# A drain instruction raises TensorE's three increments in a counting sort that four engines share

## The reference, cut to what matters

```python
edge_mats = (bond_features @ W_bond + b_bond).reshape(-1, d, d)
h = atom_features
for _ in range(STEPS):                      # 4
    msg = jnp.einsum('eij,ej->ei', edge_mats, h[nbr])
    agg = jax.ops.segment_sum(msg, dst, num_segments=n_atoms)
    h = _gru_cell(agg, h, W_ih, W_hh, b_ih, b_hh)
...
deg = jax.ops.segment_sum(jnp.ones_like(edge_weight), col, num_segments=num_nodes)
norm = deg_inv_sqrt[row] * edge_weight * deg_inv_sqrt[col]
out = jax.ops.segment_sum(x[row] * norm[:, None], col, num_segments=num_nodes)
...
h = relu(layernorm(x)); x = x + L0(h, ...)
h = relu(layernorm(x)); x = x + L1(h, ...)
```

## Time and profile before

| | us |
|---|---|
| median of three runs without the profiler | 27782.18 |
| profiled execution, span | 33286.7 |
| sort, from the first to the last L645 | 771.8 to 6977.5 |
| POOL busy in the span | 20140.3 |

### The profile page before, as it was taken

The page is one execution under the profiler, slowest core; times in us unless marked ns, Lnnn a source line. Parts: engine busy times, 40 slices in busy tenths (PEclk is TensorE's granted clock), DMA queues, the critical chain, the costliest instruction groups (busy, mean ns, idle before and its releaser), DMA issues. The chain is left out here.

```text
span 33286.7 us, 248524 instructions
## 1 busy us (share of the span) xinstructions
PE 12311.8 (37%) x67675; PEld 9311.2 (28%) x67676; DVE 9799.0 (29%) x17458; ACT 4841.4 (15%) x12143; POOL 20140.3 (61%) x20823
## 2 busy tenths in 40 slices
PE   5433334434444434444444444444444441000003
PEld 4222222223333333333333333333333330000003
DVE  8555555532222222222222222212222221000006
ACT  7222222211111111111111111111111110000003
POOL 0444444456666656666656666665666666777772
PEclk7666666667677667776666677666777775555555
DMA  3111111111111111111111111111111111111113
GB/s 147 56 60 60 60 60 60 60 36 25 24 25 25 24 22 25 24 25 25 25 22 25 25 24 25 25 22 24 25 24 25 25 24 35 40 40 40 40 40 79
DMA packets 1804969, 1246.48 MB, mean 37 GB/s; under 512 B 1170117, under 2 KB 1735346, under 8 KB 1780271
## 3 DMA queue, kind: packets, MB, share of 16 engines
q1 hardware_dynamic: 574528, 850.03, 8.4%
q0 software_dynamic: 666016, 324.92, 7.2%
q10 hardware_dynamic: 564300, 70.11, 1.4%
HBM read 957.69 MB, written 285.80 MB: 37 GB/s over the span
## 5 line engine op out<-in xcount | busy, mean ns | idle before, releaser
L1081 POOL DMA_INDIRECT h_rows<-h_table,rec x13680 | 12939.7, 946 | 6987.6 <-issue 4190.7
L1231 PE MATMUL outer<-a_masked,h_by_quarter 128*128 128x136 f32 x27360 | 5353.3, 371 | 11179.8 <-DVE h_by_quarter L1122 9823.8
L1231 PEld LDWEIGHTS outer<-a_masked,h_by_quarter 128*128 128x128 f32 x27360 | 5063.9, 272 | 11661.2 <-issue 11293.4
L855 POOL DMA_INDIRECT edges_by_node<-row,place x3125 | 3001.8, 961 | 3159.4 <-DVE row L784 2245.4
L1277 ACT COPY outer_sums<-outer 128x408 f32<-128x408 f32 x4560 | 2171.4, 502 | 17391.6 <-PE outer L1231 7933.1
L1498 POOL DMA_INDIRECT messages_by_bucket<-ms,ix x3420 | 3621.6, 1059 | 1189.7 <-issue 1168.5
L1115 DVE TENSOR_TENSOR a_masked<-rec,gates 128x2040 f32<-128x2040 f32 x912 | 2073.5, 2274 | 6823.6 <-remote 5115.6
L1122 DVE TENSOR_TENSOR h_by_quarter<-h_rows,gates 128x1920 f32<-128x1920 f32 x912 | 1963.2, 2153 | 6720.6 <-DMA h_rows<-h_table,rec 6671.5
L1207 PE MATMUL msg_psum<-outer_sums,w_bond_blocks 128*128 128x480 f32 x7752 | 3544.3, 604 | 0.0
L1207 PEld LDWEIGHTS msg_psum<-outer_sums,w_bond_blocks 128*128 128x128 f32 x7752 | 1594.8, 217 | 1415.8 <-issue 1415.8
L645 PE MATMUL nextf<-o_hi,o_lo 128*128 128x98 bf16 x3125 | 499.7, 231 | 3359.4 <-ACT next_free L700 1997.0
(11 more groups left out here) (276 smaller groups left out, 11907.3 us busy)
## 6 DMA issues: line engine op xcount, KB each, us to landing
h_rows<-h_table,rec POOLq DMA_INDIRECT x13680
key_row<-source_keys SPq DMA_DIRECT2D x125, 1600.0 KB
rec<-edges_by_node SPq DMA_DIRECT2D x1140, 157.5 KB
low_key_row<-source_low_keys SPq DMA_DIRECT2D x126, 800.0 KB
carry_flags<-carry_flags SPq DMA_DIRECT2D x285, 240.0 KB
mr<-messages_by_bucket SPq DMA_DIRECT2D x220, 264.0 KB, 2.7
messages_by_bucket<-zeros SPq DMA_DIRECT2D x36, 1600.0 KB, 36.7
chunk_sums<-scan_t ACTq DMA_DIRECT2D x912, 60.0 KB
```

The costliest lines, as they stand in the source:

```text
L855: pool.indirect_dma_start(out=r3, out_offset=bass.IndirectOffsetOnAxis(ap=place[b][:, u:u + 1], axis=0), in_=row[b][:, u, :], in_offset=No ...
L1081: pool.indirect_dma_start(out=hb[j][:, u, :], out_offset=None, in_=ht, in_offset=bass.IndirectOffsetOnAxis(ap=rec[j][:, u, W_DST:W_DST + 1 ...
L1231: last = pe.matmul(pt[(j * NB + g) % RING][:, at:at + KC], hq[j % 2][:, u, :, :].rearrange("p q d -> p (q d)"), am[j % 2][:, u, :, :].rear ...
```

## The change

In the sort, the last matmul before each of the three increments no longer carries it. A drain instruction stands behind the matmuls and carries the increment in its place. It is one drain behind L636, one behind each batch's L645 group, and one behind the step's last L652: five a step, 3125 in all. Matmuls, waits and their order are the same. Line numbers behind L637 move up by one in the changed kernel.

```diff
                             pe.matmul(nextb[:, 0:SW], before_b[:], dst_tiles(at, S), start=False, stop=False,
-                                      skip_group_check=True).then_inc(s_bx, 1)
+                                      skip_group_check=True)
+                            pe.drain().then_inc(s_bx, 1)
...
                                 for j in range(j0, j1):
-                                    last = pe.matmul(nextf[:, 0:HB], o_lo[b][:, s * S + j, :], o_hi[b][:, s * S + j, :], start=False, stop=False,
-                                                     skip_group_check=True)
-                                last.then_inc(s_add, 1)
+                                    pe.matmul(nextf[:, 0:HB], o_lo[b][:, s * S + j, :], o_hi[b][:, s * S + j, :], start=False, stop=False,
+                                              skip_group_check=True)
+                                pe.drain().then_inc(s_add, 1)
                                 if k == 0:
                                     pe.wait_ge(s_lr, t + 1)
                                     hold(pe)
                                 for j in range(j0, j1):
-                                    last = pe.matmul(plook[(b + s) % 2][:, j * HB:(j + 1) * HB], ot_f[b][:, s * S + j, :], nfs[k][:],
-                                                     start=True, stop=True, skip_group_check=True)
-                            last.then_inc(s_look, 1)
+                                    pe.matmul(plook[(b + s) % 2][:, j * HB:(j + 1) * HB], ot_f[b][:, s * S + j, :], nfs[k][:],
+                                              start=True, stop=True, skip_group_check=True)
+                            pe.drain().then_inc(s_look, 1)
```

## The result

The changed kernel took 27946.86 us (four runs, 27938.33 to 27975.97), the kernel before 27782.97 us (27779.33 to 27784.53) beside it. The ratio is 1.0061, with a 95% interval of 1.0049 to 1.0073: slower by 164 us. The direction and the range held; the size did not, 577 us had been forecast.

The account below looks back on a forecast made before the run. POOL's 31.6 us a sort iteration was taken as the bound; drains would make TensorE's 36.0 us the bound, 4.4 us over, 550 us in 125 iterations. With 580 us taken, the forecast was 28360 us, range 27950 to 28940.

Parts of the forecast that it names:

- What bounds the kernel: Sort, timed runs: an iteration is the longer of POOL's 31.6 us and DVE's 29.7 us.
- The 5504 us are not in the timed runs: Profile against timed runs: late increments come with the profiler; sort waits of 2256 us and message-step waits of 2743.6 us explain 5000.
- late in both, and drains on top: TensorE's queue in the sort: late increments are real and hold drains too, 750 us more, 28530 us; chance 0.12.
- The sum for a step: TensorE's step in the sort: with the drains 7.2 us at the lower clock, 4.95 us at the full one.
- The drains' share: TensorE's step, lower clock: five drains add 1.5 us, at 0.30 us each, plus 0.6 us for instructions no longer hidden.
- small instructions: TensorE's queue behind drains: waits, register instructions and holds, formerly hidden by matmuls, cost 0.6 us a step, between 0 and 1.2.
- So I expect the lower clock nearly always: TensorE in the sort: stays at the lower clock, so 36.0 us an iteration, 4.4 over POOL's 31.6, 550 us in all.
- The size: Whole kernel: 580 us slower, taken between 550 us with POOL as the bound and 790 us with DVE.
- Full cover at the full clock: Sort at the full clock: TensorE's 24.8 us an iteration stays under POOL's 31.6 us, so the change costs nothing.
- Faster, by increments that the sequencer raises in time: Sort: late increments are real and drains avoid them; an iteration falls from 49.65 to 36.0 us, 26080 us; chance 0.17.

## Why the prediction was right in sign and wrong in size

- *What bounds the kernel.* Held. POOL's 31.6 us an iteration is 31.56 in the kernel before, and DVE's 29.7 is 29.17 with half the scatters.
- *The 5504 us are not in the timed runs.* The conclusion held, the reason did not: I laid them to the profiler, and they go with the chip. That the result came from a chip of the first kind was luck. On the other kind my rival "late in both, and drains on top" came true: 945 us, where I had 750, and POOL's mean period went from 49.0 to 57.1 us (traces of two chips), by 8.1, where I had 6.
- *The sum for a step.* The drains' share held; the step that it was added to was a little short. At the lower clock I had 5.08 + 2.1 = 7.2 us, start to start, and 7.36 to 7.40 was measured. The step of 5.08 us in the earlier trace rows ends at the full clock: its last lookups take 0.51 us, where they take 0.71 at the lower one. The same trace has steps wholly at the lower clock, and they take 5.24 us (a window from one L633 to the next, columns as in the earlier trace rows):

```profile
1021.48:1026.72 5.24, 5.24 (x22) 3.66 (x21) 4.70 (x19) 2.49 (x7) 0.00 (x0) 0.50 0.00 0
```

So the five drains cost 7.36 - 5.24 = 2.12 us. At the full clock I had 3.05 + 1.9 = 4.95 us; 4.48 of its own was measured, and 4.70 start to start. The split was near too. Where nothing stands behind a drain, the next matmul starts 0.08 us behind the end that the trace gives for the last one (2166.12 + 0.37 to 2166.57). Behind the drains of `s_bx`, the first `s_add` and `s_look` the array is idle 0.45, 0.32 and 0.23 us, and what these stand over the 0.08, 0.37 + 0.24 + 0.15 = 0.76 us a step, is my estimate of the small instructions there from this trace, where I had 0.6.
- *"So I expect the lower clock nearly always."* This is the step that failed. The term was 36.0 - 31.6 = 4.4 us in every iteration, 550 us; it came to 33.13 - 31.58 = 1.55 us, 192 us over 124 iterations of the profiled execution and 164 us in the median. TensorE was at the lower clock for 304 of some 600 steps only, and at the full one, where the cover holds, for 148. The 30 iterations that were at the lower clock nearly throughout took 35.7 to 37.6 us, where the sum has 36.0. I had argued from a stretch with 4.59 of 6 us busy that stayed low. In the changed kernel a stretch with 30.39 of 36 us busy stayed low too, where I had 5 of 7.2, and yet in between the full clock came back for a few steps at a time; what brings it back was not shown. The filler run shows that with the clock at 0.90 nothing of the loss is left.
- *The size.* The forecast put 580 us, between that 550 and a 790 for which DVE would have been the bound, and that bound did not apply: POOL's period without the drains is 31.56 us.
- *Full cover at the full clock.* Held: the filler run is at the time of before.
- *Faster, by increments that the sequencer raises in time.* Did not come: on the chips with late increments the drains are late with them. That the queue stands at a drain until the matmuls ahead of it have ended is in the trace: in the changed kernel, from 940 to 4940 us, the first matmul behind a drain starts at the least 0.07 us behind the end of the one ahead of it, where the earlier trace rows have an overlap of 0.20 us. On the chips with late increments the drains last up to 15.6 us (16.5 behind L636).
- *Open.* What moves the 73 us between the changed kernel and the one with increments left on the matmuls is open. Their steps are equally long and differ in how many fell to the full clock; whether the signal or chance sets that was not shown, since no later run was on a chip of the first kind. The same holds for four drains. What makes some chips late is open too.

## What to carry to other kernels

Here a stop in TensorE's queue cost more than the overlap of the matmuls: of the 2.12 us that five drains added to a step at the lower clock, 0.76 us are my estimate for small instructions, which in the kernel before left the overlap of 0.20 us between matmuls as it was. Whether such a stop costs time was decided in the long iterations (up to 37.6 us) and not in the mean (33.1), and those were the ones at TensorE's lower clock: price a change at both clocks (here 7.36 to 7.40 and 4.70 us a step), and take neither as given. And compare a profile's own time with the timed runs before its waits are believed; where they differ by a sixth, a second profile answers more than any row of the first.

## What had not been expected

- Two kinds of chips: 27783 us and 33256 to 33482 us for one kernel, and on the second increments of matmuls and drains 12 to 15 us late while POOL scatters.
- Work added made the kernel faster: 3125 filler matmuls took the changed kernel from 27947 to 27783 us with the granted clock in the sort at 0.90 in place of 0.65.
- The drain behind L636 lengthened a step at the lower clock by 0.7 us, the three behind L645 by 1.15 us together. Of the 0.7 us 0.37, and of the 1.15 us 0.24, are by the estimate above for the small instructions behind the drain.
